# Key roundings of the weight folding and the latent rows of the last two pairs of cross attention: a new order on three engines

## What is computed

```python
x = x + _L0_xattn_ref(_layernorm(x, axis=-1), ctx_2048, mask_BxS2_bk0)
...
q = x @ wq_a_w.T + wq_a_b                      # 384 columns
q = rmsnorm(q, q_norm_w)
q = q @ wq_b_w.T + wq_b_b                      # split in q_nope, q_pe
kv_full = x @ wkv_a_w.T + wkv_a_b              # 128 + 64 columns
kv, k_pe = (kv_full[..., :KVLR], kv_full[..., KVLR:])
k_pe = k_pe * cos[None] + rotate_half(k_pe) * sin[None]
q_nope = jnp.einsum('bshd,hdc->bshc', q_nope, wkv_b[:, :NOPE])
kv = rmsnorm(kv, kv_norm_w)
```

## Time and profile before

| what | value |
|---|---|
| median of 3 runs | 1090.47 us (1090.14 to 1091.06) |
| the profiled execution | 1090.33 us, of which the span of instructions is 1088.5 us |
| mean granted TensorE clock | 0.997 |
| TensorE busy | 1063.1 us of the span (98%) |
| VectorE, ScalarE, GpSimd busy | 508.1, 338.9, 294.9 us |

### The profile page before, as it was taken

The page is one execution under the profiler, slowest core; times in us unless marked ns, Lnnn a source line. Parts: engine busy times, 40 slices in busy tenths (PEclk is TensorE's granted clock), DMA queues, the critical chain, the costliest instruction groups (busy, mean ns, idle before and its releaser), DMA issues.

```text
span 1088.5 us, 18667 instructions
## 1 busy us (share of the span) xinstructions
PE 1063.1 (98%) x7233; PEld 904.0 (83%) x7233; DVE 508.1 (47%) x914; ACT 338.9 (31%) x630; POOL 294.9 (27%) x341
## 2 busy tenths in 40 slices
PE   5999989999999999999999999999999999999997
PEld 3677777788888888888888888999999898989896
DVE  3666556545555554445455668532324232414232
ACT  3565554422222222223222236312222221313030
POOL 2434363321112101131112102423233232415050
PEclk9999999999999999999999999999999999999999
DMA  9999962200022000320012072200101010101000
GB/s 359 414 418 394 404 230 87 74 20 21 20 68 88 20 19 14 107 58 20 20 59 88 20 252 90 77 20 20 39 1 40 1 39 0 39 0 40 1 21 20
DMA packets 40851, 101.26 MB, mean 93 GB/s; under 512 B 7049, under 2 KB 11172, under 8 KB 36292
## 3 DMA queue, kind: packets, MB, share of 16 engines
q1 hardware_dynamic: 39044, 96.62, 24.9%
q10 hardware_dynamic: 1728, 3.54, 0.8%
HBM read 74.45 MB, written 17.30 MB: 84 GB/s over the span
## 4 chain that ended last, share of the span: by engine, by line
PE 95%; DVE 2%; issue 1%; DMA 1%; POOL 1%; ACT 0%; SPq 0%; POOLq 0%; DVEq 0%; ACTq 0%
PE b_z L44 6%; PE b_z L46 6%; PE b_z L45 6%; PE b_score L44 5%; PE b_score L46 5%; PE b_prob L46 5%; PE b_score L45 5%; PE b_prob L44 5%; PE b_prob L45 5%; PE b_turn L44 4%; PE b_turn L46 4%; PE b_turn L45 4%; PE b_read L46 4%; PE b_read L44 4%; PE b_read L45 4%; PE b_read L619 2%
## 5 line engine op out<-in xcount | busy, mean ns | idle before, releaser
L1505 POOL TENSOR_TENSOR f_hT_lo<-f_h,f_hT_hi 128x512 fp32r<-128x512 f32 x64 | 92.4, 1444 | 106.2 <-ACT f_hT_hi L1550 96.9
L812 POOL TENSOR_TENSOR m_sc<-m_sc,m_rs 128x1024 f32<-128x1024 f32 x16 | 30.5, 1905 | 241.9 <-DVE m_rs L975 241.9
L1606 DVE TENSOR_TENSOR f_h<-f_h 128x512 f32<-128x512 f32 x64 | 49.7, 777 | 91.4 <-ACT f_h L1545 91.1
L44 PE MATMUL b_z<-m_zT_lo,m_wq_hi 128*128 128x512 f32 x192 | 75.0, 390 | 1.0 <-issue 0.7
L45 PE MATMUL b_z<-m_zT_hi,m_wq_lo 128*128 128x512 f32 x192 | 74.7, 389 | 0.0
L46 PE MATMUL b_z<-m_zT_hi,m_wq_hi 128*128 128x512 f32 x192 | 74.7, 389 | 0.0
L44 PE MATMUL b_turn<-f_xnT_lo,f_up_hi 128*128 128x256 f32 x256 | 72.6, 283 | 0.0
L44 PE MATMUL b_read<-f_xnT_lo,f_up_hi 128*128 128x256 f32 x256 | 72.5, 283 | 0.0
L45 PE MATMUL b_read<-f_xnT_hi,f_up_lo 128*128 128x256 f32 x256 | 72.4, 283 | 0.0
L46 PE MATMUL b_read<-f_xnT_hi,f_up_hi 128*128 128x256 f32 x256 | 72.4, 283 | 0.0
L46 PE MATMUL b_turn<-f_xnT_hi,f_up_hi 128*128 128x256 f32 x256 | 72.4, 283 | 0.0
(11 more groups left out here) (268 smaller groups left out, 3098.7 us busy)
## 6 DMA issues: line engine op xcount, KB each, us to landing
x_ctx_in<-ctx_rows_dram SPq DMA_DIRECT2D x16, 1024.0 KB, 15.0
x_ctxT<-ctx_turned_dram SPq DMA_DIRECT2D x15, 1024.0 KB, 14.9
m_swapped<-m_by_sin SPq DMA_DIRECT2D x128, 64.0 KB, 2.0
m_raw<-attn_raw_dram SPq DMA_DIRECT2D x6, 768.0 KB, 10.6
m_z_in<-z_scratch SPq DMA_DIRECT2D x4, 1152.0 KB, 5.7
x_x_all<-x_dram SPq DMA_DIRECT2D x16, 256.0 KB, 15.7
m_x<-x_scratch SPq DMA_DIRECT2D x4, 1024.0 KB, 6.0
x_scratch<-m_x SPq DMA_DIRECT2D x4, 1024.0 KB, 4.7
```

Of the source, the lines that this page charges most:

```text
L44: nc.tensor.matmul(out, lh, rl, start=first, stop=False)
L812: q.tensor_tensor(e, e, rs[:].unsqueeze(2).broadcast_to([P, HB, SEQ]), ALU.mult).then_inc(s["normed"], 1)
L1505: g.tensor_tensor(hT_lo[:, 2 * n:2 * n + 2].rearrange("p m n -> p (m n)"), h[:, n % 2], hT_hi[:, 2 * n:2 * n + 2].bitcast(F32).rearrange(" ...
L1606: v.tensor_tensor(h[:, n % 2], h[:, n % 2], h[:, n % 2], ALU.mult).then_inc(s["squared"], 1)
```

## The change

No instruction is added, taken away or altered; TensorE and SyncE keep their order. Three lists are reordered.

- GpSimd: the rotation of pair 14 is put ahead of `rope_lo(0)`, and `rope_hi(1)` ahead of `latent_rstd(15)`.
- ScalarE: `squares(14)` is put ahead of `keys_hi(4)`, `squares(15)` ahead of `keys_hi(8)`.
- VectorE: `latent_var(14)` is put ahead of `keys_lo(4)`, `latent_kv(14)` ahead of `bias(15)`, `latent_var(15)` ahead of `keys_lo(8)`.

```diff
--- before.py
+++ after.py
@@ -1789,10 +1789,10 @@
             x["rotate"](L - 2, L % 2)
             w["rope_hi"](0)
             x["latent_rstd"](L - 1)
+            x["rotate"](L - 1, 1 - L % 2)
             w["rope_lo"](0)
-            x["rotate"](L - 1, 1 - L % 2)
+            w["rope_hi"](1)
             x["latent_rstd"](L)
-            w["rope_hi"](1)
             x["rotate"](L, L % 2)
             w["rope_lo"](1)
             m["groups"]()
@@ -1818,13 +1818,14 @@
             x["scale_q"](L - 2, L % 2)
             w["keys_hi"](2)
             w["keys_hi"](3)
+            x["squares"](L - 1, 1 - L % 2)
             w["keys_hi"](4)
-            x["squares"](L - 1, 1 - L % 2)
             x["scale_q"](L - 1, 1 - L % 2)
-            for f in range(5, 9):
+            for f in range(5, 8):
                 w["keys_hi"](f)
             x["squares"](L, L % 2)
-            w["keys_hi"](9)
+            for f in range(8, 10):
+                w["keys_hi"](f)
             x["scale_q"](L, L % 2)
             for f in range(10, weights.KEY_FILLS):
                 w["keys_hi"](f)
@@ -1892,14 +1893,15 @@
             x["latent_kv"](L - 2, L % 2)
             w["keys_lo"](2)
             w["keys_lo"](3)
+            x["latent_var"](L - 1)
             w["keys_lo"](4)
-            x["latent_var"](L - 1)
+            x["latent_kv"](L - 1, 1 - L % 2)
             x["bias"](L, L % 2)
-            x["latent_kv"](L - 1, 1 - L % 2)
-            for f in range(5, 9):
+            for f in range(5, 8):
                 w["keys_lo"](f)
             x["latent_var"](L)
-            w["keys_lo"](9)
+            for f in range(8, 10):
+                w["keys_lo"](f)
             x["latent_kv"](L, L % 2)
             for f in range(10, weights.KEY_FILLS):
                 w["keys_lo"](f)
```

## The result

| | before | changed |
|---|---|---|
| median | 1090.47 us (1089.09 to 1091.06, 7 runs) | 1086.47 us (1085.76 to 1087.73, 7 runs) |
| ratio | | 0.9966 (95% interval 0.9954 to 0.9978) |
| profiled execution, and its span | 1090.33, 1088.5 | 1087.06, 1085.3 |

The change is faster by 3.7 us by the ratio (2.4 to 5.0). 1086.8 was predicted.

A forecast was written before the change was run, and what follows sets the result against it. TensorE, busy 98% of the span, was taken as the bound. Gains of 2.1 us (wait) and 1.5 us (clock) bring the span from 1088.5 to 1084.9; plus 1.8 and 0.1 gives 1086.8 us, range 1085.9 to 1089.3.

The forecast's parts named there:

- The wait: TensorE ahead of fill 9: its wait for `keys_lo(5)` falls from 3.70 to 1.6 us, a gain of 2.1.
- the collision: VectorE's `latent_kv(14)` (L491) starts inside GpSimd's `rope_lo(0)` and is held until 0.15 us behind its end; shortened, not removed.
- The clock: TensorE's fills 9 to 11: after a wait of 1.6 us the clock stays at 1.00, gaining 1.5 us.
- the sum: Whole kernel: 2.1 us (wait) + 1.5 us (clock) = 3.6 us gained.
- The most that can be had: At fills 9 to 11 on TensorE: wait and slow fills together allow 5.20 us, no more.
- Pair 15: Value fills and second `latent_kv`: `latent_kv(15)` passes 0.7 us ahead of `rope_lo(1)`; third value fill late by 0.1 at most.
- The cause of the wait: Fill 9's 3.70 us wait: `keys_lo(5)` is late because `latent_kv(14)` is held by `rope_lo(0)`.
- A: Fills 9 to 11: the clock falls all the same, costing 1.5 us; gain 2.1, 1088.4 us; chance 0.11.
- B: Second `latent_kv`: held by `rope_lo(1)`, value fills stand 3.3 us, 1.3 slower, 1091.8 us; chance 0.08.
- C: Behind `rope_lo(0)`: `rope_hi(1)` goes ahead of L491, 1.4 us later; 1089.8 to 1088.3 us; chance 0.06.
- D: Value fills or stage_m: another gate moves the wait instead of shortening it; 1090 to 1090.5 us; chance 0.07 with others.

The follow-up runs named there:

- pool_old: The changed kernel with GpSimd back in its old order: 1085.88 us, ratio 0.9956 to the kernel before.
- bias_first: The changed kernel with `bias(15)` ahead of `latent_kv(14)` on VectorE, as before: 1086.21 us, ratio 0.9958 to the kernel before.
- rope_late: The changed kernel with `rope_lo(0)`, `rope_hi(1)` and `rope_lo(1)` behind the rotation of pair 15 on GpSimd: 1084.84 us, ratio 0.9947 to the kernel before.
- before_filler: The kernel before, with 12 matmuls that nobody reads between fills 8 and 9 on TensorE: 1090.01 us, ratio 0.9996 to the kernel before.
- delay2: The changed kernel with two idle VectorE statistics instructions between `bias(15)` and `keys_lo(5)`: 1088.48 us, ratio 0.9984 to the kernel before.
- collide2: The changed kernel with `latent_kv(15)` one rounding later on VectorE, behind the start of `rope_lo(1)`: 1089.64 us, ratio 0.9995 to the kernel before.
- pair15_old: The changed kernel with `squares(15)` and `latent_var(15)` each back behind rounding 8: 1087.08 us, ratio 0.9973 to the kernel before.
- before_rope_late: The kernel before, with only `rope_lo(0)`, `rope_hi(1)` and `rope_lo(1)` moved behind the rotation of pair 15 on GpSimd: 1087.13 us, ratio 0.9972.

## Why the prediction was right

**The wait.** I had L491 end 0.15 behind `rope_lo(0)`, 1.6 us of wait left and 2.1 gained. It ended 0.15 behind (160.40 and 160.25), the wait is 1.37, and 2.33 is gained. Of the 0.2 between the two, 0.13 is the step over `bias(15)`: I took 0.86 from the old trace, where L491 behind it began no sooner than `q_rstd` was there (ScalarE's L429, which waits for it, starts at the same 159.41); without that wait it is 0.73 (160.32 to 161.05). The rest is hundredths. pool_old, bias_first and rope_late each end the hold of L491 sooner or put less behind it, and TensorE's wait follows: 1.14, 0.72 and 1.37 us less. That the collision holds VectorE is shown: L491 took 1.92, 0.78, 1.20 and 2.78 us where it started inside `rope_lo`, ending 0.15 behind it each time, and 0.34 where it did not. The rule of the Trainium skill's page "SBUF — State Buffer", section "Who interferes with whom", that the one to start first keeps the ports to its end (the page calls the lock exclusive and says "for the whole instruction" of VectorE's 2-port modes), holds in all of these.

**The clock.** I took a cost of 0 after a wait of 1.6, between two rows, by nearness. Right here: 2.76 us for the three fills, 1.41 less than before, where I had 1.50, since the first fill behind any wait takes 0.97 to the next and not 0.89. So the two terms measured 2.33 and 1.41, 3.74 together, where the sum had 3.6. before_filler shows that the standing still is the cause of the slow fills. That a wait of this length would leave the clock up was a choice and no working: what decides it I could not say, and delay2 and collide2 do not settle it.

**What the sum passed over.** before_filler also shows this: I added 1.50 as if it were a loss by itself, and before the change only 0.60 of it was, since a gate behind it stood ready. The sum came out right because the change moves that gate too (`squares(15)` and `latent_var(15)` ahead of rounding 8, `rope_hi(1)` ahead of `latent_rstd(15)`). The prediction did not count on this, so here it was lucky, by 0.6 us as pair15_old measures it.

**The most that can be had.** I put it at 5.20 us; rope_late gained 5.32. I counted the wait from the end of fill 8, but a fill that does not wait starts 0.16 ahead of that end (159.93 against 159.03 + 1.06 in rope_late). The same slip stands in the sentence that fill 9 would not wait at all without the collision: with `keys_lo(5)` ending at 159.9 it would have been due at 159.86, and late by some 0.2.

**Pair 15.** I looked at this part only for what it could spoil, and found 0.7 us of room ahead of `rope_lo(1)`; it is 0.67. That it brings 0.6 us of its own (pair15_old) the prediction did not say. It had followed `latent_kv(15)` and not `scale_q(15)`, behind which ScalarE's `keys_hi(10)` stands.

**The cause of the wait.** I put all of the old 3.70 on the collision. It was the last gate, but with it taken away alone 1.50 us of the wait stayed, for another gate, ScalarE's `scale_q(14)` with `keys_hi(5)` behind it (before_rope_late). The change moves `squares(14)` and `latent_var(14)` early enough to take that one away, so the sum did not suffer. I followed the new chain on ScalarE and never asked what it had been worth in the old one.

**Rivals.** A (clock falls all the same) did not happen in the traces of the changed kernel and its repeat; the 13 times of both lie within 2 us, at mean granted clocks of 0.998 and 0.999. B is real but 0.67 us away, and cost less in collide2 than I priced it (3.1 us over the changed kernel by the medians, 5.0 by my numbers), since its wait was 2.19 and not 3.3. C did not happen: L491 got in ahead of the queued `rope_hi(1)`, ending 0.15 behind L1368. D did not: the distance and the ratio agree.

## What to carry to other kernels

Where a VectorE instruction with two inputs in SBUF lies behind a long two-input GpSimd instruction, look at its duration in the trace: the maximum of ten times the median was here a wait that no list of waits named. The cure that gave all, together with the new order on ScalarE and VectorE, was to put the long GpSimd work where no such instruction is due, not to finish it sooner. And when a wait is explained, ask which gate comes second, by taking the first away alone: here the second gate was worth 1.5 of 3.7 us, and the slow clock hid 0.8 us of another.

## What the runs showed that I had not expected

- A wait of 2.55 us left the clock at 1.00 (delay2, profiled execution), and one of 2.19 us was followed by 0.51 (1.2 GHz), within 1.2 us after TensorE had begun again (collide2, profiled execution). In the kernel before it fell while TensorE still stood: 0.65 is the mean of 163.10 to 163.73. The mean clocks of the other executions of delay2 and collide2 suggest that both outcomes occur in both kernels. What tells them apart stays open.
- 12 matmuls that nobody reads, put into a wait of 3.7 us, made the three fills behind it 1.4 us faster and the kernel no slower.
- `rope_lo`, 3.45 us long, took the same time with a VectorE instruction held behind it (156.80 in the changed kernel) as without (163.33 in rope_late): the one that came first paid nothing.
